# Delta stage: a chunk's triangle solved in three TensorE rounds over 16x16 diagonal inverses, in place of one round over the whole 32x32 inverse

## What is computed

```python
kb = kc * bc[:, None]
A = jnp.tril(kb @ kc.T, -1)
U = solve_triangular(eye + A, vc * bc[:, None] - kb @ S, lower=True)
o = qc @ S + jnp.tril(qc @ kc.T) @ U
return (S + kc.T @ U, o)
```

## Time and profile before

| | us |
|---|---|
| median of 3 runs (1423.44 to 1427.81) | 1425.33 |
| span of the profiled execution | 1419.9 |
| busy in it: VectorE | 1131.7 |
| TensorE | 996.3 |
| GpSimd | 789.5 |
| ScalarE | 685.8 |

### The profile page before, as it was taken

How to read it: one execution, slowest core, us unless ns; L and a number is a source line. 1 busy time by engine, 2 the same in 40 slices (tenths; PEclk the granted TensorE clock), 3 DMA queues, 4 the chain that set the end, 5 groups by cost and what they waited for, 6 DMA issues and landing times.

```text
span 1419.9 us, 32994 instructions
## 1 busy us (share of the span) xinstructions
PE 996.3 (70%) x11963; PEld 734.6 (52%) x11963; DVE 1131.7 (80%) x3199; ACT 685.8 (48%) x1510; POOL 789.5 (56%) x668
## 2 busy tenths in 40 slices
PE   4537768678785556399999955655455599999960
PEld 1214455545554445278888842323223378888850
DVE  1188899998999874389888846999999889788845
ACT  2444354452533212177777734444444277777740
POOL 3232256666565452527777651167777647777660
PEclk9778779586785655599999986777766599999985
DMA  5010101111111114149788832011211549788839
GB/s 134 23 45 25 47 24 59 37 50 46 55 58 37 49 32 164 37 138 307 253 292 281 282 117 92 30 63 63 68 38 34 194 160 296 252 282 287 280 110 350
DMA packets 78625, 184.34 MB, mean 130 GB/s; under 512 B 16735, under 2 KB 44826, under 8 KB 68224
## 3 DMA queue, kind: packets, MB, share of 16 engines
q1 hardware_dynamic: 51280, 142.04, 29.7%
q0 software_dynamic: 17280, 35.70, 7.2%
q10 hardware_dynamic: 9904, 4.49, 1.2%
HBM read 131.20 MB, written 52.79 MB: 130 GB/s over the span
## 4 chain that ended last, share of the span: by engine, by line
DVE 34%; PE 32%; POOL 12%; issue 10%; ACT 5%; DMA 4%; SPq 1%; POOLq 0%; DVEq 0%; ACTq 0%
PE ps L1539 5%; POOL res L668 4%; DVE seq L1172 4%; POOL xs L630 4%; PE ps L1747 2%; PE ps L1748 2%; PE ps L1749 2%; POOL rn L613 2%; PE ps L1761 2%; PE ps L1759 2%; PE ps L1760 2%; DVE prod L787 2%; DVE t_p L791 2%; DVE r_stats L709 2%; DMA res<-orow,idt 2%
## 5 line engine op out<-in xcount | busy, mean ns | idle before, releaser
L630 POOL DMA_INDIRECT xs<-ysc,slot_u x256 | 281.4, 1099 | 186.7 <-DVE slot_u L930 114.7
L668 POOL DMA_INDIRECT res<-orow,idt x284 | 292.3, 1029 | 144.7 <-issue 79.2
L1094 DVE TENSOR_TENSOR hidl<-hidf,hidh 128x512 fp32r<-128x512 f32 (+1 forms) x320 | 199.2, 637 | 21.1 <-ACT hidh L1408 15.1
L1406 ACT ACTIVATE hidf<-ps,wb 128x512 f32<-128x512 f32 (+1 forms) x320 | 198.3, 654 | 4.2 <-PE ps L1749 3.7
L1747 PE MATMUL ps<-yTh,wb 128*128 128x512 f32 (+1 forms) x320 | 126.3, 395 | 0.0
L1759 PE MATMUL ps<-hidh,wb 128*128 128x512 f32 (+1 forms) x320 | 124.5, 389 | 0.0
L1749 PE MATMUL ps<-yTh,wb 128*128 128x512 f32 (+1 forms) x320 | 119.2, 372 | 0.0
L1748 PE MATMUL ps<-yTl,wb 128*128 128x512 f32 (+1 forms) x320 | 119.1, 372 | 0.0
L1761 PE MATMUL ps<-hidh,wb 128*128 128x512 f32 (+1 forms) x320 | 117.8, 368 | 0.0
L1760 PE MATMUL ps<-hidl,wb 128*128 128x512 f32 (+1 forms) x320 | 117.4, 367 | 0.0
L1416 ACT ACTIVATE out_t<-ps,wb 128x512 f32<-128x512 f32 (+1 forms) x80 | 51.3, 642 | 111.9 <-PE ps L1761 111.9
(11 more groups left out here) (259 smaller groups left out, 2573.4 us busy)
## 6 DMA issues: line engine op xcount, KB each, us to landing
wb<-wblob SPq DMA_DIRECT2D x80, 1032.0 KB, 5.6
xt<-xs SPq DMA_DIRECT2D x62, 288.0 KB
wblob<-hl SPq DMA_DIRECT2D x16, 512.0 KB
fin<-res SPq DMA_DIRECT2D x14, 512.0 KB, 10.3
hidf<-res SPq DMA_DIRECT2D x10, 512.0 KB, 4.1
res<-orow,idt POOLq DMA_INDIRECT x284
xs<-ysc,slot_u POOLq DMA_INDIRECT x256
rs<-res SPq DMA_DIRECT2D x8, 512.0 KB, 4.7
```

Of the source, the lines that this page charges most:

```text
L630: pool.indirect_dma_start(xs[:, :], bass.IndirectOffsetOnAxis(slot_u[:, g % 2, k, n:n + 1], 0), ysc[:, g % 2, n, :], None).then_inc(s(f"mo ...
L668: pool.indirect_dma_start(res[m][:, :], bass.IndirectOffsetOnAxis(idt[:, t % IR, j:j + 1], 0), orow[:, t % OR, j, :], None, bounds_check=2 ...
L1094: ve.tensor_tensor(hidl[:, t % 2, c, 0:n], hidf[:, t % 2, c, 0:n], hidh[:, t % 2, c, 0:n].bitcast(F32), ALU.subtract)\
L1406: ins = act.activation(hidf[:, t % 2, c, 0:n], ps[:, c, 0:n], ACT.Gelu_apprx_tanh, bias=b_col)
```

## The change

The whole inverse is no longer made. VectorE keeps the row-by-row part for the two 16x16 diagonal blocks and turns the result back in slot 16; the eight steps for the block below the diagonal and all their instructions go. Each chunk is instead solved on TensorE in three rounds of 32 small matmuls: first the diagonal inverses times `R`, copied to `y1` by ScalarE; then the block below the diagonal (rows 0 to 15 of `n_c`) times `y1`, added to the lower halves of `R` by VectorE; then the diagonal inverses times this `R`. All four chunks of a group are solved in the iteration of its inverse, at slots 17, 23, 29 and 35. So that `R` needs no product with beta, keys times minus beta (`kb`) are made, and are transposed besides `kn` and `qn`; the values go from the projection's PSUM into `R` on ScalarE. `n_c` is a plain ScalarE copy of the Gram matrices. The transposed `wk` goes to the solve's own bank.

```diff
-        kn = sb1("kn", [3, BPB, KW])
+        kb = sb1("kb", [3, BPB, KW])
...
+        y1 = sb1("y1", [2, HEADS, RH])
...
-        A_RV = 24
-        A_RK = 24
-        A_KQT = (22, 26)
-        A_GRAM = (34, 35, 36, 40)
+        A_KQT = (22, 24, 26)
+        A_GRAM = (33, 35, 37, 39)
         B_INV = 1
-        B_SECOND = (16, 18, 22, 25, 26, 28, 29, 32)
-        B_TC = 34
-        UW = ((35, 38), (9, 18))
-        WT = ((36, 41), (11, 22))
-        C_AT = (2, 11, 24, 29)
+        B_TC = 16
+        UW = (17, 23, 29, 35)
+        U_Y1, U_Z, U_ADD, U_X, U_OUT, U_T = 1, 2, 2, 4, 4, 5
+        C_AT = (2, 11, 20, 29)
...
+        WT0 = 2 * HEADS * RH
...
+                keys = kn[:, :, :].rearrange("p n (h d) -> p n h d", d=DK)
+                if t == A_KN:
+                    ve.wait_ge(s("d_rn"), g + 1)
+                    ve.tensor_tensor(keys, kq[:, :, 0:KW].rearrange("p n (h d) -> p n h d", d=DK),
+                                     bc(rn[:, :, 0:HEADS], 3, DK), ALU.mult).then_inc(s("d_kn"), 1)
                     marks["beta"] = ch.mark(ve.tensor_scalar(nbeta[:, :, :], th[:, :, :], -0.5, -0.5, ALU.mult, ALU.add))
-                for half in range(GPB):
-                    hb = slice(half * GB, (half + 1) * GB)
-                    if t == A_RV + half:
-                        ch.wait(marks["beta"])
-                        if g >= 2:
-                            ve.wait_ge(s("d_uwp"), (g - 1) * CG)
-                        ve.tensor_tensor(R[:, g % 2, hb, :, 0:DV],
-                                         kqv[:, hb, V0:V0 + HEADS * DV].rearrange("p n (h d) -> p n h d", d=DV),
-                                         bc(beta[:, hb, :], 3, DV), ALU.mult)
-                if t == A_RK:
-                    ve.wait_ge(s("d_kn"), 2 * g + 1)
-                    ve.tensor_tensor(R[:, g % 2, :, :, DV:RH], kn[:, g % 3].rearrange("p n (h d) -> p n h d", d=DK),
-                                     bc(beta[:, :, :], 3, DK), ALU.mult).then_inc(s("d_R"), 1)
+                if t == A_KN + 1:
+                    ch.wait(marks["beta"])
+                    ve.wait_ge(s("d_kn"), 3 * g + 1)
+                    ve.tensor_tensor(kb[:, g % 3].rearrange("p n (h d) -> p n h d", d=DK), keys,
+                                     bc(nbeta[:, :, :], 3, DK), ALU.mult).then_inc(s("d_kn"), 1)
+                    if g >= 2:
+                        ve.wait_ge(s("d_uwp"), (g - 1) * CG)
+                    ve.tensor_copy(R[:, g % 2, :, :, DV:RH], keys).then_inc(s("d_R"), 1)
...
-                    ve.wait_ge(s("d_gram"), g * CG + c + 1)
+                    ve.wait_ge(s("d_nc"), g * CG + c + 1)
                     both = slice(2 * c, 2 * c + 2)
-                    grams = ps[:, 0:4, 0:P].rearrange("p b (h z t) -> p b h z t", h=2, z=2)
-                    ve.tensor_tensor(n_c[:, both].rearrange("p n (a h) t -> p (n a) h t", h=2), grams[:, :, :, 0],
-                                     bc(nbeta[:, both].rearrange("p n (a h) -> p (n a) h", h=2), 3, C), ALU.mult)
...
-                    ve.wait_ge(s("d_gp"), (g + 1) * CG)
-                    ve.transpose(n_p[:, :, :].rearrange("p i l -> p l i"), n_c[:, :, :, :].rearrange("p n h j -> p j (n h)")).then_inc(s("d_np"), 1)
+                    ve.wait_ge(s("d_nc"), (g + 1) * CG)
+                    ve.transpose(n_p[:, :, :], n_c[:, :, :, :].rearrange("p n h j -> p j (n h)"))\
+                        .then_inc(s("d_np"), 1)
...
-                k = B_SECOND.index(t) if t in B_SECOND else -1
-                if 0 <= k < 4 and step == 0:
-                    m0, n = 4 * k, SUB - 4 * k
-                    ch.wait(marks["row"])
...
+                for c in range(CG):
+                    if t == UW[c] + U_ADD:
+                        rows = R[:, g % 2, 2 * c:2 * c + 2].rearrange("p n h d -> p (n h d)")
+                        ve.wait_ge(s("d_zp"), g * CG + c + 1)
+                        ve.scalar_tensor_tensor(rows, ps[:, BK_B, 0:2 * HEADS * RH], head_of[:, 1, 0:1], rows, ALU.mult, ALU.add).then_inc(s("d_z"), 1)
...
-                    act.copy(kqv[:, n, :], ps[:, bank, 0:G0])
+                    act.copy(kq[:, n, :], ps[:, bank, 0:KQ])
+                    act.copy(R[:, g % 2, n, :, 0:DV], ps[:, bank, V0:G0].rearrange("p (h d) -> p h d", d=DV))
...
+                if t in A_GRAM:
+                    c = A_GRAM.index(t)
+                    act.wait_ge(s("d_gram"), g * CG + c + 1)
+                    if g >= 1:
+                        act.wait_ge(s("d_np"), g)
+                        act.wait_ge(s("d_zp"), (g - 1) * CG + c + 1)
+                    grams = ps[:, 0:4, GR0:GR0 + P].rearrange("p b (h z t) -> p b h z t", h=2, z=2)
+                    act.copy(n_c[:, 2 * c:2 * c + 2].rearrange("p n (a h) t -> p (n a) h t", h=2),
+                             grams[:, :, :, 0]).then_inc(s("d_nc"), 1)
+
+            def first_part(g, c):
+                act.wait_ge(s("d_y1p"), g * CG + c + 1)
+                act.wait_ge(s("d_zp"), g * CG + c)
+                act.copy(y1[:, :, :, :].rearrange("p n h d -> p (n h d)"), ps[:, BK_B, 0:2 * HEADS * RH]).then_inc(s("d_y1"), 1)
...
+            def apply(g, t):
+                for c in range(CG):
+                    if t == UW[c] + U_Y1:
+                        first_part(g, c)
+                    if t == UW[c] + U_OUT:
+                        applied(g, c)
+                    if t == UW[c] + U_T:
+                        turned_w(g, c)
...
+            def solve(g, c, what):
+
+                def columns(n, h):
+                    k0 = (n * HEADS + h) * RH
+                    return slice(k0, k0 + RH)
+
+                for n in range(2):
+                    for h in range(HEADS):
+                        for q in range(Q):
+                            out = ps[rows_of(q), BK_B, columns(n, h)]
+                            if what == "below":
+                                top = slice(C * q, C * q + SUB)
+                                ins = pe.matmul(out, n_c[top, 2 * c + n, h, :], y1[top, n, h, :],
+                                                start=True, stop=True, skip_group_check=True)
+                            else:
+                                ins = pe.matmul(out, t_c[rows_of(q), 2 * c + n, h, :], R[rows_of(q), g % 2, 2 * c + n, h, :],
+                                                start=True, stop=True, skip_group_check=True)
+                return ins
+
+            def apply(g, t):
+                for c in range(CG):
                     at = g * CG + c
+                    if t == UW[c]:
                         pe.wait_ge(s("d_R"), g + 1)
                         pe.wait_ge(s("d_inv"), g + 1)
+                        pe.wait_ge(s("d_wTs"), at)
+                        pe.wait_ge(s("d_kqv"), min(g + 2, B) * BPB)
+                        solve(g, c, "first").then_inc(s("d_y1p"), 1)
+                    if t == UW[c] + U_Z:
+                        pe.wait_ge(s("d_y1"), at + 1)
+                        solve(g, c, "below").then_inc(s("d_zp"), 1)
+                    if t == UW[c] + U_X:
+                        pe.wait_ge(s("d_z"), at + 1)
+                        solve(g, c, "whole").then_inc(s("d_uwp"), 1)
+                for c in range(CG):
+                    at = g * CG + c
+                    if t == UW[c] + U_T:
                         pe.wait_ge(s("d_uw"), at + 1)
+                        pe.transpose(ps[:, BK_B, WT0:WT0 + P], wk[:, c % 2].rearrange("p n d -> p (n d)"), ident[:, :])\
                             .then_inc(s("d_wT"), 1)
```

More of the change, by code:

```diff
@@ L1301, in turned_w @@
                 act.wait_ge(s("d_wT"), g * CG + c + 1)
-                act.copy(wT[:, g % 2, c, :], ps[:, BK_O, 0:P]).then_inc(s("d_wTs"), 1)
+                act.copy(wT[:, g % 2, c, :], ps[:, BK_B, WT0:WT0 + P]).then_inc(s("d_wTs"), 1)
             def stage_c(g, t):
@@ L1578, in stage_a @@
                     ins.then_inc(s("d_gram"), 1)
-            def apply(g, late, t):
-                for k in range(2):
-                    c = 2 * late + k
+            def solve(g, c, what):
[14 more added lines that the diff above has]
+                return ins
```

124 lines of the change are left out of this document (38 added, 86 removed).

## The result

The changed kernel takes 1528.39 us (median of 4 runs, 1523.99 to 1530.06) against 1426.23 beside it: ratio 1.0719, 95% interval 1.0694 to 1.0744. It is slower, as forecast, but by 102 us in place of 56, and above the range.

The account below looks back on a forecast made before the run. VectorE was taken to bound the kernel; the change makes one chain A to D, 69 us against 60.1. Losses of 36 (middle four), 14 (first two) and 6 (last two), in all 56, gave 1481 us, range 1446 to 1520.

Parts of the forecast that it names:

- A: Start of `n_p` to end of `t_c`: the unchanged 22.90 and the transpose's 1.96, 24.9 us.
- B: End of `t_c` to end of `kn`: low-clock first round, logits, choice, `y1`, round below and state matmuls, 12.8 us.
- C: From TensorE's release at 36.6 to the first convolution: transposes, rounds and ScalarE copies in a chain, 12.5 us, to 49.1.
- D: First convolution to next `n_p`: two convolutions at 3.70, solves, Gram matmuls and output in a chain, 19.4 us, to 68.5.
- I take the high clock from here: From the start of C, TensorE's instructions priced at the high clock, except the transposes of `y` at 1.11 us.
- I take 7: First two iterations, without routing: each loses between nothing and 8.9 us, taken as 7, together 14.
- 3 each: Last two iterations, without convolution: bounds -4 and +8 us, taken as a loss of 3 each, together 6.
- a shorter list on VectorE alone would shorten the iteration: Middle four iterations: VectorE is the full engine, busy 223.60 of 240.30 us; the change takes 14.8 an iteration off it.
- The low clock up to the first convolution: Rival: TensorE stays low, C takes 18.6 and the first convolution 6.28, 77 us an iteration, 1533 in all; chance 0.15.
- The high clock throughout: Rival: the solve fills TensorE's gaps and its clock stays up, 64.5 us an iteration, 1447 in all; chance 0.17.
- The faster case: Rival: engines overlap and the fullest sets the pace, saving 7 us in each of 8 iterations, 1369; chance 0.07.
- The drain at a change of tiling mode: TensorE's switches between 128-row matmuls and 32x32 tiles: priced at nothing; at 0.1 us each, 11 us, making 1492.

Follow-up runs that it names:

- warm: Changed kernel plus 29 matmuls of 128x128 by 256 columns that nobody reads, in TensorE's waits ahead of chunk 0's round below, middle iterations; 1523.46 us, ratio 1.0687.
- late places: Changed kernel with only the last of three rounds, chunks 2 and 3 solved in the next iteration; 1468.44 us, weights' cast in slot 6 1470.51, in slot 15 1445.09.
- five orders: Five complete versions of the changed kernel with work moved into waits that the profile showed; 1568.45, 1524.58, 1566.13, 1593.45 and 1542.88 us.
- the burst: Changed kernel plus 640 small matmuls that nobody reads, in TensorE's wait ahead of chunk 1's update in two middle iterations; 1583.85 us, one profiled run.
- early keys: Changed kernel with logits ahead of chunk 0's first round and the transposes of `y`, `kn` and its transposes in earlier slots; 1524.58 us, ratio 1.0696.
- two banks: Changed kernel with logits first, chunks 0 and 1 solved interleaved in two PSUM banks, chunks 2 and 3 five slots earlier; 1542.88 us, ratio 1.0839.
- the slowest three: Changed kernel with chunks 2 and 3 solved late, 1568.45 us; that with logits, keys and `y` transposes early, 1566.13; the latter with the second convolution last, 1593.45.

## Why the prediction was right and wrong

**Right: the order, and the first half of the iteration.** The forecast's pieces in the four middle iterations, measured:

| piece | forecast | measured |
|---|---|---|
| A, to the end of `t_c` | 24.9 | 24.71, 24.75, 26.82, 24.69 |
| B, to the end of `kn` | 12.8 | 12.65 in all four |
| C, to the first convolution | 11.5 | 12.48, 15.66, 13.49, 15.01 |
| D, to the next `n_p` | 19.4 | 23.42, 25.04, 22.03, 25.00 |

The forecast's "12.5" for C counts from TensorE's release at 36.6; from the end of `kn` at 37.6, where the measured C is cut, it leaves 11.5.

The `n_p` transposes stand 73 to 78 us apart, not 66 to 71. The other marks that it named are there: VectorE 42 busy, `kn` 37 after `n_p` (once 39), rounds of 1.50 near the logits, idle times ahead of `lg`, of the additions and, by `gp` behind ScalarE's `n_c`, of `n_p`:

```profile
384.04 0.23 DVE L857 COPY lg<-ps 128x64 f32<-128x64 f32 x1 [4.88 <-PE ps L1685]
...
388.47 0.62 DVE L796 SCALAR_TENSOR_TENSOR R<-ps,head_of,R 128x384 f32<-128x384 f32 x1 [1.44 <-PE ps L1582]
...
426.72 0.42 DVE L761 TENSOR_TENSOR gp<-ps,m_p 128x256 f32<-128x256 f32 x1 [0.71 <-ACT n_c L1271]
```

**Wrong: the term D, "19.4", and with it C, "12.5".** D measured 23.9 in the mean, 17.9 us too little over four iterations; C 14.2 against 11.5, 10.6 too little. The step that failed is "I take the high clock from here". In C the granted clock was 0.91, 0.72, 0.88 and 0.73 over the four iterations, and C was 12.48, 15.66, 13.49 and 15.01. The two convolutions of D were put at 3.70 each, the price of the second one in the earlier trace rows:

```profile
327.03 4.73 PE L1530 MATMUL ps<-yT,tap 128*128 128x512 f32 x8
...
337.96 6.07 PE L1530 MATMUL ps<-yT,tap 128*128 128x512 f32 x8 [0.59 <-ACT hS L1222]
...
416.55 3.67 PE L1530 MATMUL ps<-yT,tap 128*128 128x512 f32 x8 [0.81 <-ACT hS L1222]
```

Over the four iterations the first took 3.69, 4.73, 4.98 and 5.33, the second 5.44, 6.07, 3.67 and 6.10: 2.6 us of D's 4.5 in the mean. The rest was not itemised; the sum left out `gp` (0.42) ahead of `n_p` and the waits at each hand-over. In the two iterations shown, the one with pauses of 0.96 and 1.17 us in C has C at 15.66 and a clock of 0.72; the other, with pauses of at most 0.21, 13.49 and 0.88. That the pauses bring the low clock is read from these rows and from `warm`, and was not shown by taking a pause away. It cannot be all: in the fourth iteration a round of scores times `vp` runs at the low clock (1.09 us) with no pause ahead of it in C. Nor did any run show D at the high clock throughout; in `warm` it is 24.1 in the mean.

**Wrong: the outer iterations.** "I take 7" for each of the first two was 13.5 and 10.4: the bound of 8.9 was itself the middle's loss, and came out with it. "3 each" for the last two, 6 in all, was 19.8 for all that follows the middle. Together these miss 24 of the 52 us; the four middle iterations miss 27.

**Wrong, but without weight in the sum: "a shorter list on VectorE alone would shorten the iteration".** The earlier trace rows show TensorE at 14.47 of 19.41 and 17.05 of 19.07 in the two later parts, beside VectorE's 18.73 and 15.65. I read one full engine where a second was nearly full; without the eight steps the kernel gained 1.1%.

**The rivals.** The low clock up to the first convolution gave 1533, next to the result, for a reason that did not occur: it had C at 18.6 and the convolution at 6.28. The clock in C was 0.72 to 0.91, and raising the mean clock gained 5 us, within the intervals. The high clock throughout (1447) fails already in B, at 0.50 in all four iterations and 12.65 long. The faster case needed everything behind `t_c` under 35.2 us; it takes 48 to 53. The drain at a change of tiling mode (1492 in the prediction) was not tested by itself.

## What to carry to other kernels

Before work is moved from a full engine to another, cut the iteration into its parts and ask which engine is full in the part where the work would land: a second full engine makes the removed work worth little (15 of 118 us here) and the added work cost about its own time (44 us for 45.9). Price a step of many small matmuls by three terms, the array's time, the pace at which the instructions come (28 ns a record here), and the hand-overs of its chain; here the copy, the addition and the hand-overs, with the lower clock that came with them, cost about as much as the work on TensorE (40 and 44 us). A place that looks idle on one engine can be the one stretch where another has no wait, as VectorE's rows were here. After each new order, look for an instruction that has nothing to do with the change and has begun to wait: the weights' cast spoiled two runs of the late places, and five orders were timed with it.

## What was not expected of the hardware

In the burst TensorE's small matmuls came in packs of 128 records with pauses of up to 2.44 us, 3.64 us a pack in the mean, though a pack ran in 1.56 us. Each pack is one packet of 256 instructions. Some orders lengthened the pauses, from 21.3 us with the change to 31.7 with early keys and 34.2 with two banks; the slowest three did not (18.1 to 22.2). And the clock, raised from 0.791 to 0.833 by matmuls that nobody reads, was worth 5 us of 1528, within the spread.
